# Second expert's weights loaded a phase earlier, its first matrix split in halves and its tokens transposed inside the first expert's first product

## The chip, the cores and the metric

One core of a Trainium2 chip runs the whole program. The metric is the device time of one execution in microseconds (us); the time of a kernel is the median of its runs.

## The reference, cut to what matters

A cross attention is added to `x` (32 batches of 256 tokens, width D = 256). Behind it stands a layer of E = 16 experts. Every expert takes the 512 tokens of the 8192 whose router logit for it is highest, so every expert has the same amount of work:

```python
logits = xn @ router_weight.T + router_bias
_, idx = jax.lax.top_k(logits.T, top_k)                  # 16 x 512
xe = xn[idx]
h = jnp.einsum('ecd,efd->ecf', xe, fc1_weight) + fc1_bias[:, None, :]   # F = 1024
h = jax.nn.gelu(h, approximate=False)
y = jnp.einsum('ecf,edf->ecd', h, fc2_weight) + fc2_bias[:, None, :]
contrib = (y * gates[:, :, None]).reshape(-1, d)
output = jnp.zeros(...).at[flat_idx].add(contrib)        # scatter-add, gates normalised
```

## The kernel before, in words

The program is four phases, one block each, with all engines meeting between two blocks.

- `attention_phase` (to about 540 us of the span): attention, router logits, and a table of normalised rows in HBM.
- `search_phase` (L779, 540 to 632 us): VectorE (DVE) looks for every expert's threshold by bisection, with one small matmul per step. Beside it SyncE (SP) loads expert 0's two weight matrices (L818, L820), ScalarE (ACT) copies them to a rounded high part (`W1H`, `W2H`, L847), and GpSimd (POOL) subtracts to get the low part (`W1L`, `W2L`, L835). Each part is announced by a semaphore (`w1h_ready`, `w1l_ready`, and the same for w2).
- `slots_phase` (L976, to 716 us): from thresholds to lists of token indices. At its end POOL gathers the tokens and gates of experts 0 and 1 (`XG`, `G`, L1050, L1056).
- `expert_phase` (L1162, from 716 us): the 16 experts.

All products of the expert phase are made in three passes (high x high, low x high, high x low; `three`, L1451). For an expert e of the pair (i, u), e = 2i + u, TensorE (PE) does: `columns` (L1441), 8 transposes of the gathered tokens into `xt_bank`; `up` (L1456), the first product in KF = 8 groups f of 6 matmuls of 512 columns, group f using columns f*128 to f*128+127 of `W1H` and `W1L`, with four PSUM banks in turn; `down` (L1469), the second product, 96 matmuls of 256 columns. PE's order is written out at L1484: columns(0), up(0), columns(1), up(1), columns(2), down(0), and then up(e), columns(e+1), down(e-1) for each further expert.

The other engines follow orders of their own:

- ACT (L1394): `hidden` makes for each group f the GELU from PSUM (`HF`, L1421) and, one group later, the rounded copy of group f-1 (`HH`, L1415). Between the hidden parts of two experts stands `split_1(e)` (L1398), one copy of the whole `W1` (2048 elements per partition) to `W1H`, and, from expert 2 on, `split_2(e-1)` (L1404).
- DVE (L1279): `columns` (L1302) scales the transposed tokens to a high part `XTH` (L1306) and a low part `XTL` (L1310). `split_1` (L1290) makes `W1L` (L1294). `hidden` (L1321) subtracts for each group to get `HL` (L1326). `indices` (L1281) copies index lists for POOL, `keep_gates` (L1314) saves the gates, `contributions` (L1329) turns the second product into the scaled output rows. The written order at the start (L1359) is columns(0), keep_gates(0), hidden(0), split_1(1), indices(2), columns(1), keep_gates(1), hidden(1), and then `turn` (L1347) for each expert: split_1(e), indices(e+1), columns(e), contributions(e-2), keep_gates(e), split_2(e-1), hidden(e).
- SP (L1202): waits for `w1l_ready` and loads `W1` of expert 1 (L1206), two bias rows (L1217), `W2` of expert 1 (L1211), and then for each further expert load_1(e), load_2(e), load_b(e). One buffer holds the raw `W1`, one the raw `W2`: the load of the next expert waits until the low part of the last one is made.
- POOL (L1229): gathers the tokens of experts 2, 3, ... (L1238, L1242) and scatter-adds finished rows (L1253), in turn.

The three lines that hold PE back between up(0) and up(1) are, on PE,

```python
            pe.wait_ge(xt_ready, e + 1)
            pe.wait_ge(w1l_ready, e + 1)
```

and on ACT, ahead of the copy that `W1L` is made from,

```python
                act.wait_ge(h_done, KF * e)
```

Of the kernel before, what the change touches and what calls it, by code (L numbers as in the profile page):

```python
# [4 lines left out]
FP32 = mybir.dt.float32  # L5
# [5 lines left out]
ALU = mybir.AluOpType  # L11
ACT = mybir.ActivationFunctionType
AX = mybir.AxisListType

P = 128
B, S, D = 32, 256, 256
M = 120
H, DH = 16, 16
# [5 lines left out]
F = 1024  # L24
KF = F // P
# [753 lines left out]
def search_phase(nc, ctx, sem, bank, ident, L, probs, front, w1T, b1, w2T, nw, same_e, same_e_below, same_e16, zero_row):  # L779
# [36 lines left out]
    @block.sync  # L816
    def _(sp):
        sp.dma_start(front["W1"][:, :, :], w1T[0:1, :, :].rearrange("o (k p) f -> p (o k) f", p=P)) \  # L818
            .then_inc(front["w1_loaded"], 16)
        sp.dma_start(front["W2"][:, :, :], w2T[0:1, :, :].rearrange("o (k p) d -> p (o k) d", p=P)) \  # L820
            .then_inc(front["w2_loaded"], 16)
        sp.dma_start(front["NW"][:, :], nw).then_inc(front["c_loaded"], 16)
        sp.dma_start(front["B1"][:, :], b1).then_inc(front["c_loaded"], 16)

    @block.gpsimd
    def _(pool):

        pool.wait_ge(mx_ready, 1)
        pool.tensor_tensor(expl[:, :, :], L[:, :, :], mx[:, :, :].to_broadcast([P, NT, E]), ALU.subtract) \
            .then_inc(lx_ready, 1)  # L830
        pool.wait_ge(ex_ready, 1)
        sum_experts(pool, tree, expl, sum_ready)
        for w in ("1", "2"):
            pool.wait_ge(front[f"w{w}h_ready"], 1)
            pool.tensor_tensor(front[f"W{w}L"][:, :, :], front[f"W{w}"][:, :, :], front[f"W{w}H"][:, :, :].bitcast(FP32),  # L835
                               ALU.subtract).then_inc(front[f"w{w}l_ready"], 1)
        pool.wait_ge(rsm_ready, 1)
        pool.tensor_tensor(probs[:, :, :], expl[:, :, :], rsm[:, :, :].to_broadcast([P, NT, E]), ALU.mult) \
            .then_inc(probs_ready, 1)

    @block.scalar
    def _(act):
        act.wait_ge(lx_ready, 1)
        act.activation(expl[:, :, :], expl[:, :, :], ACT.Exp).then_inc(ex_ready, 1)
        for w in ("1", "2"):
            act.wait_ge(front[f"w{w}_loaded"], 16)
            act.activation(front[f"W{w}H"][:, :, :], front[f"W{w}"][:, :, :], ACT.Copy).then_inc(front[f"w{w}h_ready"], 1)  # L847

    @block.vector
    def _(dve):  # L850
# [311 lines left out]
def expert_phase(nc, ctx, sem, bank, ident, front, idx, gate_table, xn_table, w1T, w2T, b2, out):  # L1162
# [39 lines left out]
    @block.sync  # L1202
    def _(sp):
        def load_1(e):
            sp.wait_ge(w1l_ready, e)
            sp.dma_start(W1[:, :, :], w1T[bass.ds(e, 1), :, :].rearrange("o (k p) f -> p (o k) f", p=P)) \  # L1206
                .then_inc(w1_loaded, 16)

        def load_2(e):
            sp.wait_ge(w2l_ready, e)  # L1210
            sp.dma_start(W2[:, :, :], w2T[bass.ds(e, 1), :, :].rearrange("o (k p) d -> p (o k) d", p=P)) \  # L1211
                .then_inc(w2_loaded, 16)

        def load_b(e, u, first=False):
            if not first:
                sp.wait_ge(y0_ready, e - 1)
            sp.dma_start(B2[u][:, :], b2[bass.ds(e, 1), :].to_broadcast([P, D])).then_inc(b2_loaded[u], 16)  # L1217

        load_1(1)
        load_b(0, 0, True)  # L1220
        load_b(1, 1, True)
        load_2(1)
        with sp.Fori(1, E // 2) as i:
            for u in range(2):
                load_1(2 * i + u)
                load_2(2 * i + u)
                load_b(2 * i + u, u)
# [52 lines left out]
    def _(dve):  # L1280
# [6 lines left out]
            dve.tensor_copy(II[u][:, :], idx[:, bass.ds(e, 1), 0, :].rearrange("p o g -> p (o g)"))  # L1287
            dve.tensor_copy(IG[u][:, :], idx[:, bass.ds(e, 1), 2, :].rearrange("p o g -> p (o g)")).then_inc(idx_ready, 1)  # L1288

        def split_1(e, first=False):  # L1290
            dve.wait_ge(w1h_ready, e + 1)
            if not first:
                dve.wait_ge(h_done, KF * e)
            dve.tensor_tensor(W1L[:, :, :], W1[:, :, :], W1H[:, :, :].bitcast(FP32), ALU.subtract).then_inc(w1l_ready, 1)  # L1294

        def split_2(e, first=False):
            dve.wait_ge(w2h_ready, e + 1)
# [20 lines left out]
            dve.wait_ge(gates_gathered[u], 16 * GT * (i + 1))  # L1318
            dve.tensor_copy(GK[u][:, :], G[u][:, :]).then_inc(gk_ready, 1)

        def hidden(i, u):  # L1321

            e = 2 * i + u
            for f in range(KF):
                dve.wait_ge(hh_ready, KF * e + (f + 1))
                dve.tensor_tensor(HL[u][:, f, :], HF[f % 4][:, :], HH[u][:, f, :].bitcast(FP32), ALU.subtract) \  # L1326
                    .then_inc(hl_ready, 1)
# [19 lines left out]
        def turn(i, u, ahead=True, first=False):  # L1347

            e = 2 * i + u
            split_1(e)  # L1350
            if ahead:
                indices(i + u, 1 - u, isinstance(e, int) and e == 2)
            columns(i, u)
            contributions(i - 1, u, first)
            keep_gates(i, u)
            split_2(e - 1)
            hidden(i, u)

        dve.wait_ge(c_loaded, 32)  # L1359
        columns(0, 0)  # L1360
        keep_gates(0, 0)
        hidden(0, 0)
        split_1(1)
        for g in range(E // EG):
            dve.wait_ge(ids_moved[g], 16 * EG)
        indices(1, 0, True)
        columns(0, 1)
        keep_gates(0, 1)
        hidden(0, 1)
        turn(1, 0, first=True)  # L1370
# [24 lines left out]
    def _(act):  # L1395
        act.wait_ge(c_loaded, 32)

        def split_1(e, first=False):  # L1398
            act.wait_ge(w1_loaded, 16 * (e + 1))
            if not first:  # L1400
                act.wait_ge(h_done, KF * e)
            act.activation(W1H[:, :, :], W1[:, :, :], ACT.Copy).then_inc(w1h_ready, 1)  # L1402

        def split_2(e, first=False):  # L1404
            act.wait_ge(w2_loaded, 16 * (e + 1))
# [4 lines left out]
        def hidden(i, u, first):  # L1410
            e = 2 * i + u

            def high(f):
                act.wait_ge(hf_ready, KF * e + (f + 1))
                act.activation(HH[u][:, f, :], HF[f % 4][:, :], ACT.Copy).then_inc(hh_ready, 1)  # L1415

            for f in range(KF):
                act.wait_ge(h_done, KF * e + (f + 1))
                if not isinstance(e, int) or e > 0 or f >= 4:
                    act.wait_ge(hl_ready, KF * e + (f - 3))  # L1420
                act.activation(HF[f % 4][:, :], h_bank[f % 4][:, :], ACT.Gelu,  # L1421
                               bias=B1[:, bass.ds(KF * e + f, 1)]).then_inc(hf_ready, 1)
                if f == 0 and not first:
                    act.wait_ge(y_done, e - 1)
                if f:
                    high(f - 1)
            high(KF - 1)

        hidden(0, 0, True)
        split_1(1)  # L1430
        hidden(0, 1, True)
        with act.Fori(1, E // 2) as i:
            for u in range(2):
                split_1(2 * i + u)
                split_2(2 * i + (u - 1))
                hidden(i, u, False)
        split_2(E - 1)
# [2 lines left out]
    def _(pe):  # L1440
# [12 lines left out]
            pe.matmul(o, wh, xl, start=False, stop=False)  # L1453
            return pe.matmul(o, wl, xh, start=False, stop=last)  # L1454

        def up(i, u, first):  # L1456
            e = 2 * i + u
            pe.wait_ge(xt_ready, e + 1)
            pe.wait_ge(w1l_ready, e + 1)
            for f in range(KF):  # L1460
                if not first or f >= 4:
                    pe.wait_ge(hf_ready, KF * e + (f - 3))
                for k in range(KD):
                    w = slice(f * P, (f + 1) * P)
# [17 lines left out]
            ins.then_inc(y_done, 1)  # L1482

        columns(0, 0, True)  # L1484
        up(0, 0, True)
        columns(0, 1, False)
        up(0, 1, False)
        columns(1, 0, False)
        down(0, 0, True)
# [74 lines left out]
```

## Time and profile before

| | us |
|---|---|
| median of 3 runs | 1132.67 |
| lowest, highest | 1127.72, 1132.79 |
| the profiled execution, its own time | 1131.91 |
| its span, first to last instruction | 1129.9 |
| PE busy in the span | 910.2 (81%) |
| DVE busy | 802.1 (71%) |
| POOL busy | 593.0 (52%) |
| ACT busy | 512.5 (45%) |

The profiled execution lies 2.0 us above its span and 0.76 us below the median. In the page's forty slices of 28 us each, PE stands at nine tenths through the attention, is near idle in the search, and is at nine tenths again from slice 28 to the end; the granted clock of TensorE is at half speed in between. A row of a timeline gives start, duration, engine, line, operation, output and inputs, the number of instructions merged, and in brackets how long the engine had been idle before and what ended that. Matmuls overlap in the records, so their pace is read from start to start, not from the duration of one. A row of a table by windows gives the stretch and its length, then the busy time of PE, of PE's weight loads, of DVE, ACT and POOL (with instruction counts), the granted clock as a share of 2.4 GHz, the share of the DMA engines and GB/s.

### The profile page before, as it was taken

The page shows a single profiled execution, that of the slowest core. Times are in us where ns is not written, and L with a number is a line of the kernel's source. Part 1 is how long each engine was busy: PE and PEld are TensorE (multiplying, and loading weights), DVE is VectorE, ACT ScalarE, POOL GpSimd, SP SyncE. Part 2 cuts the span into 40 slices and gives each one's busy share as a digit, 9 for nine tenths or more (in the row PEclk, how much of TensorE's full clock was granted, in tenths as well). Part 3 has the DMA queues.
Part 4 walks back from the last instruction along what each step waited for, and adds up shares of the span by engine and source line. Part 5 has one row for each costly group of instructions (what it writes and reads, how often), then busy time and mean ns, then how long its engine had stood idle before and what let it go on. Part 6 is the DMA issues. An engine that isn't in the chain of part 4 may idle for free. (4 is left out here: it accounts for less than half of the span.)

```text
span 1129.9 us, 22145 instructions
## 1 busy us (share of the span) xinstructions
PE 910.2 (81%) x7028; PEld 730.0 (65%) x7028; DVE 802.1 (71%) x1586; ACT 512.5 (45%) x872; POOL 593.0 (52%) x558
## 2 busy tenths in 40 slices
PE   4899999999999999986100054779999999999984
PEld 3566666666766666754000054669888999889974
DVE  4677888888888888872799899356666566665742
ACT  1545565555555655552100112354566545665440
POOL 4245566556655665554500218125677756767524
PEclk9889999999999999996555555789999999999997
DMA  4345555555555555632200001214456654455423
GB/s 157 126 157 186 201 193 187 209 212 198 187 203 199 192 186 211 213 140 84 78 0 0 0 22 39 87 57 117 126 130 159 161 121 130 127 166 153 122 61 37
DMA packets 110948, 150.68 MB, mean 133 GB/s; under 512 B 22453, under 2 KB 80053, under 8 KB 110905
## 3 DMA queue, kind: packets, MB, share of 16 engines
q1 hardware_dynamic: 96568, 133.29, 34.1%
q0 software_dynamic: 14336, 16.82, 8.5%
q8 instruction: 26, 0.43, 0.2%
q14 instruction: 18, 0.14, 0.1%
HBM read 57.67 MB, written 25.69 MB: 74 GB/s over the span
## 5 line engine op out<-in xcount | busy, mean ns | idle before, releaser
L525 DVE TENSOR_REDUCE NM<-bank 128x4 f32<-128x480 f32 x256 | 159.7, 656 | 55.1 <-PE bank L635 54.9
L368 ACT ACTIVATE PT<-bank 120x512 f32<-120x512 f32 x256 | 139.1, 595 | 66.4 <-PE bank L660 65.7
L310 POOL TENSOR_SCALAR XN<-X,mv,rstd 128x256 f32<-128x256 f32 x128 | 155.4, 1222 | 6.9 <-POOL rstd L305 6.1
L1452 PE MATMUL bank<-W2H,HH 128*128 128x256 f32 x512 | 145.9, 285 | 5.7 <-DVE Y L1339 5.7
L1453 PE MATMUL bank<-W2L,HH 128*128 128x256 f32 x512 | 144.5, 282 | 0.0
L1454 PE MATMUL bank<-W2H,HL 128*128 128x256 f32 x512 | 144.5, 282 | 0.0
L1326 DVE TENSOR_TENSOR HL<-HF,HH 128x512 fp32r<-128x512 f32 x128 | 86.6, 691 | 70.0 <-ACT HH L1415 69.4
L1253 POOL DMA_INDIRECT out_dram<-C,IO x60 | 102.9, 1714 | 45.6 <-DVE C L1344 28.0
L1452 PE MATMUL bank<-XTH,W1H 128*128 128x512 f32 x256 | 103.9, 406 | 11.6 <-DVE XTL L1310 11.6
L635 PEld LDWEIGHTS bank<-KX,QX 128*128 128x128 f32 x512 | 73.0, 195 | 61.7 <-issue 29.0
L478 DVE RECIPROCAL RR<-RC 128x256 f32<-128x256 f32 x64 | 111.3, 1741 | 1.6 <-DMA RC<-PVS 1.5
L635 PE MATMUL bank<-KX,QX 128*128 128x240 f32 x512 | 104.2, 317 | 9.6 <-issue 4.6
L1238 POOL DMA_INDIRECT XG<-xn_table,II x56 | 54.2, 969 | 106.2 <-DVE IG L1288 93.4
L343 POOL TENSOR_TENSOR XB<-X,bp_sb 128x512 f32<-128x512 f32 x32 | 40.5, 1265 | 124.9 <-DVE X L536 124.9
L1421 ACT ACTIVATE HF<-bank,B 128x512 f32<-128x512 f32 x128 | 87.9, 687 | 34.3 <-PE bank L1454 32.6
L1454 PE MATMUL bank<-XTH,W1L 128*128 128x512 f32 x256 | 102.3, 400 | 0.0
L1453 PE MATMUL bank<-XTL,W1H 128*128 128x512 f32 x256 | 102.1, 399 | 0.0
L1452 PEld LDWEIGHTS bank<-W2H,HH 128*128 128x128 f32 x512 | 97.5, 190 | 5.9 <-DVE Y L1339 5.9
L1453 PEld LDWEIGHTS bank<-W2L,HH 128*128 128x128 f32 x512 | 97.5, 190 | 0.0
L1454 PEld LDWEIGHTS bank<-W2H,HL 128*128 128x128 f32 x512 | 97.4, 190 | 0.0
L681 PE MATMUL bank<-PT,VA 120*32 120x256 f32 x1024 | 84.0, 400 | 0.2 <-ACT PT L368 0.2
L1242 POOL DMA_INDIRECT G<-gate_table,IG x56 | 74.3, 1327 | 17.1 <-issue 16.8
(156 smaller groups left out, 1849.3 us busy)
## 6 DMA issues: line engine op xcount, KB each, us to landing
QX<-QH SPq DMA_DIRECT2D x64, 256.0 KB
W<-w1T_dram SPq DMA_DIRECT2D x16, 1024.0 KB, 8.7
W<-w2T_dram SPq DMA_DIRECT2D x16, 1024.0 KB, 5.6
KX<-KH SPq DMA_DIRECT2D x64, 240.0 KB, 2.3
X<-x_dram SPq DMA_DIRECT2D x32, 256.0 KB, 2.8
QX<-QL SPq DMA_DIRECT2D x32, 256.0 KB
RC<-PVS SPq DMA_DIRECT2D x32, 256.0 KB, 2.4
OC<-PVS SPq DMA_DIRECT2D x32, 256.0 KB, 2.6
```

Of the source, the lines that this page charges most:

```text
L310: ins = pool.tensor_scalar(dst[:, t, :], src[:, t, :], mv[:, t, 0:1], rstd[:, t:t + 1], ALU.subtract, ALU.mult)
L368: act.activation(PT[u][0:M, HE * k:HE * (k + 1), :], score_bank[k % 2][0:M, :], ACT.Exp, scale=SCALE) \
L478: dve.reciprocal(RR[:, g, :], RC[:, g, :]).then_inc(rr_ready, 1)
L525: dve.tensor_reduce(NM[u][:, t, :].rearrange("p (f n e) -> p n e f", n=HN, e=HE)[:, n, :, :], smax_bank[q % 2][:, 0:4 * M].rearrange("p (e ...
L635: ins = pe.matmul(smax_bank[q % 2][:, e * 2 * M:(e + 1) * 2 * M], QX[u][:, HE * n + e, t * P:(t + 1) * P], KX[u][:, n, :, e, :], start=Tru ...
L681: ins = pe.matmul(pv_bank[k // 2][2 * DH * c4:2 * DH * (c4 + 1), (k % 2) * S:(k % 2 + 1) * S], VA[u][0:M, h, :, :].rearrange("p d o -> p ( ...
L1253: pool.indirect_dma_start(out=out, in_=C[u][:, g, :], in_offset=None, compute_op=ALU.add, out_offset=bass.IndirectOffsetOnAxis(ap=IO[u][:, ...
L1326: dve.tensor_tensor(HL[u][:, f, :], HF[f % 4][:, :], HH[u][:, f, :].bitcast(FP32), ALU.subtract) \
L1421: act.activation(HF[f % 4][:, :], h_bank[f % 4][:, :], ACT.Gelu, bias=B1[:, bass.ds(KF * e + f, 1)]).then_inc(hf_ready, 1)
L1452: pe.matmul(o, wh, xh, start=first, stop=False)
L1453: pe.matmul(o, wh, xl, start=False, stop=False)
L1454: return pe.matmul(o, wl, xh, start=False, stop=last)
```

## The change

`W1` and `W2` of expert 1 are loaded at the end of SP's list in the search phase, as soon as the low parts of expert 0 are made, and no longer at the start of the expert phase. `w1h_ready` and `w1l_ready` now count halves, two per expert. In the expert phase `split_1` works on one half of the columns of `W1` at a time, on ACT and on DVE, and the first half needs only the first four groups of the product before. In `up`, PE waits for the first half ahead of group 0 and for the second ahead of group 4. On the first expert alone, PE does columns(1) between groups 3 and 4 of up(0); DVE does its columns(1) ahead of `HL` of group 4 and the first half of split_1(1) ahead of `HL` of group 7; ACT does its first half behind `HF` of group 6 and `HH` of group 5. From expert 2 on the two halves follow one another where the one split stood.

```diff
@@ search_phase, SP
+        sp.wait_ge(front["w1l_ready"], 2)
+        sp.dma_start(front["W1"][:, :, :], w1T[1:2, :, :].rearrange("o (k p) f -> p (o k) f", p=P)) \
+            .then_inc(front["w1_loaded"], 16)
+        sp.wait_ge(front["w2l_ready"], 1)
+        sp.dma_start(front["W2"][:, :, :], w2T[1:2, :, :].rearrange("o (k p) d -> p (o k) d", p=P)) \
+            .then_inc(front["w2_loaded"], 16)
@@ search_phase, POOL and ACT
-        for w in ("1", "2"):
-            pool.wait_ge(front[f"w{w}h_ready"], 1)
+        for w, parts in (("1", 2), ("2", 1)):
+            pool.wait_ge(front[f"w{w}h_ready"], parts)
...
@@ expert_phase, SP
-            sp.wait_ge(w1l_ready, e)
+            sp.wait_ge(w1l_ready, 2 * e)
...
-        load_1(1)
         load_b(0, 0, True)
         load_b(1, 1, True)
-        load_2(1)
@@ expert_phase, DVE
-        def split_1(e, first=False):
-            dve.wait_ge(w1h_ready, e + 1)
-            if not first:
-                dve.wait_ge(h_done, KF * e)
-            dve.tensor_tensor(W1L[:, :, :], W1[:, :, :], W1H[:, :, :].bitcast(FP32), ALU.subtract).then_inc(w1l_ready, 1)
+        def split_1(e, half):
+            fs = slice(F // 2 * half, F // 2 * (half + 1))
+            dve.wait_ge(w1h_ready, 2 * e + half + 1)
+            dve.wait_ge(h_done, KF * e - KF // 2 * (1 - half))
+            dve.tensor_tensor(W1L[:, :, fs], W1[:, :, fs], W1H[:, :, fs].bitcast(FP32), ALU.subtract).then_inc(w1l_ready, 1)
...
-        def hidden(i, u):
+        def hidden(i, u, first=False):
             for f in range(KF):
+                if first and f == KF // 2:
+                    columns(0, 1)
+                if first and f == KF - 1:
+                    split_1(1, 0)
...
-            split_1(e)
+            split_1(e, 0)
+            split_1(e, 1)
...
         columns(0, 0)
+        hidden(0, 0, True)
+        split_1(1, 1)
         keep_gates(0, 0)
-        hidden(0, 0)
-        split_1(1)
         for g in range(E // EG):
             dve.wait_ge(ids_moved[g], 16 * EG)
         indices(1, 0, True)
-        columns(0, 1)
         keep_gates(0, 1)
         hidden(0, 1)
@@ expert_phase, ACT
+        def split_1(e, half):
+            fs = slice(F // 2 * half, F // 2 * (half + 1))
             act.wait_ge(w1_loaded, 16 * (e + 1))
+            act.wait_ge(h_done, KF * e - KF // 2 * (1 - half))
+            act.activation(W1H[:, :, fs], W1[:, :, fs], ACT.Copy).then_inc(w1h_ready, 1)
...
                 if f:
                     high(f - 1)
+                if first and e == 0 and f == KF - 2:
+                    split_1(1, 0)
             high(KF - 1)
...
         hidden(0, 0, True)
-        split_1(1)
+        split_1(1, 1)
         hidden(0, 1, True)
@@ expert_phase, PE
-        def up(i, u, first):
+        def up(i, u, first, mid=False):
             pe.wait_ge(xt_ready, e + 1)
-            pe.wait_ge(w1l_ready, e + 1)
             for f in range(KF):
+                if f % (KF // 2) == 0:
+                    pe.wait_ge(w1l_ready, 2 * e + 2 * f // KF + 1)
+                if mid and f == KF // 2:
+                    columns(0, 1, False)
...
-        up(0, 0, True)
-        columns(0, 1, False)
+        up(0, 0, True, mid=True)
```

## Rows read from the trace of the kernel before

**Rows 1.** Table by windows, two stretches of the expert phase (columns as told above).
```profile
735.40:743.40 8.00, 0.08 (x1) 0.08 (x1) 6.59 (x10) 2.64 (x3) 1.74 (x2) 0.69 0.23 55
...
757.10:1097.60 340.50, 339.91 (x2225) 308.44 (x2223) 218.18 (x337) 189.08 (x255) 217.63 (x160) 1.00 0.51 131
```

**Rows 2.** Chain that ended last, 740 to 744 us: start, us, what.
```profile
740.51 1.32 DVE XTH L1306 x2
...
741.86 1.42 DVE XTL L1310 x2
...
743.32 0.80 PE bank L1452
```

**Rows 3.** Timeline of SyncE: the two loads of W1 for experts 1 and 2.
```profile
716.51 0.39 SPq L1206 DMA_DIRECT2D W<-w1T_dram  x1
...
740.53 0.41 SPq L1206 DMA_DIRECT2D W<-w1T_dram  x1
```

**Rows 4.** Timeline of ScalarE, inside and behind the first expert's product.
```profile
728.91 0.69 ACT L1421 ACTIVATE HF<-bank,B 128x512 f32<-128x512 f32 x1 [0.19 <-PE bank L1454]
729.50 0.62 ACT L1415 ACTIVATE HH<-HF 128x512 fp32r<-128x512 f32 x1
...
736.14 1.90 ACT L1402 ACTIVATE W1H<-W 128x2048 fp32r<-128x2048 f32 x1
```

**Rows 5.** Timeline of VectorE behind the first expert's product.
```profile
735.75 1.29 DVE L1326 TENSOR_TENSOR HL<-HF,HH 128x512 fp32r<-128x512 f32 x2 [0.70 <-ACT HH L1415]
738.07 2.29 DVE L1294 TENSOR_TENSOR W1L<-W,W1H 128x2048 fp32r<-128x2048 f32 x1 [1.02 <-ACT W1H L1402]
```

**Rows 6.** Timeline of TensorE: starts of up(0) and up(1), pace at either clock.
```profile
721.52 0.79 PE L1452 MATMUL bank<-XTH,W1H 128*128 128x512 f32 x1 [3.02 <-DVE XTL L1310]
...
734.08 0.39 PE L1454 MATMUL bank<-XTH,W1L 128*128 128x512 f32 x1
734.31 1.04 PE L1448 MATMUL bank<-ident,XG 128*128 128x128 f32 x8
...
743.92 0.63 PE L1453 MATMUL bank<-XTL,W1H 128*128 128x512 f32 x1
744.34 0.63 PE L1454 MATMUL bank<-XTH,W1L 128*128 128x512 f32 x1
```

**Rows 7.** Table by windows: short stretches in which the granted clock changes.
```profile
724.00:725.00 1.00, 1.00 (x5) 0.76 (x4) 0.00 (x0) 0.47 (x1) 0.00 (x0) 0.59 1.07 370
...
738.00:740.00 2.00, 0.00 (x0) 0.00 (x0) 1.93 (x1) 0.04 (x1) 0.00 (x0) 0.62 0.02 4
...
748.00:749.00 1.00, 1.00 (x4) 0.76 (x4) 0.00 (x0) 0.15 (x1) 0.69 (x2) 0.64 0.02 1
...
1097.00:1098.00 1.00, 0.67 (x6) 0.47 (x4) 0.00 (x0) 0.24 (x1) 0.00 (x0) 1.00 0.00 0
...
1100.00:1101.00 1.00, 0.00 (x0) 0.00 (x0) 1.00 (x1) 0.00 (x0) 0.00 (x0) 0.65 0.00 0
...
1116.00:1117.00 1.00, 0.76 (x7) 0.56 (x5) 0.20 (x1) 0.00 (x0) 0.98 (x1) 1.00 0.00 0
...
1120.00:1121.00 1.00, 0.00 (x0) 0.00 (x0) 0.00 (x0) 0.00 (x0) 0.80 (x1) 0.89 0.49 74
```

**Rows 8.** Timeline of GpSimd: last token gather for expert 2.
```profile
745.11 0.95 POOL L1238 DMA_INDIRECT XG<-xn_table,II  x1 [0.30 <-issue]
```

**Rows 9.** Page's list of DMA issues: count and median us to landing.
```profile
XG<-xn_table,II POOLq DMA_INDIRECT x56, 2.8
```

**Rows 10.** Chain that ended last, 792 to 817 us: around W1 of expert 4.
```profile
792.90 1.30 DVE Y L1339 x2
...
799.54 9.90 DMA W<-w1T_dram
...
816.05 0.75 DVE XTL L1310
```

**Rows 11.** Table by windows: the expert period that holds the start of up(4).
```profile
804.00:828.30 24.30, 23.71 (x154) 21.27 (x153) 15.49 (x24) 13.48 (x18) 15.71 (x12) 1.00 0.55 144
```

More of the change, by code:

```diff
@@ L832, in _ @@
         sum_experts(pool, tree, expl, sum_ready)
-        for w in ("1", "2"):
-            pool.wait_ge(front[f"w{w}h_ready"], 1)
+        for w, parts in (("1", 2), ("2", 1)):
+            pool.wait_ge(front[f"w{w}h_ready"], parts)
             pool.tensor_tensor(front[f"W{w}L"][:, :, :], front[f"W{w}"][:, :, :], front[f"W{w}H"][:, :, :].bitcast(FP32),
-                               ALU.subtract).then_inc(front[f"w{w}l_ready"], 1)
+                               ALU.subtract).then_inc(front[f"w{w}l_ready"], parts)
         pool.wait_ge(rsm_ready, 1)
@@ L844, in _ @@
         act.activation(expl[:, :, :], expl[:, :, :], ACT.Exp).then_inc(ex_ready, 1)
-        for w in ("1", "2"):
+        for w, parts in (("1", 2), ("2", 1)):
             act.wait_ge(front[f"w{w}_loaded"], 16)
-            act.activation(front[f"W{w}H"][:, :, :], front[f"W{w}"][:, :, :], ACT.Copy).then_inc(front[f"w{w}h_ready"], 1)
+            act.activation(front[f"W{w}H"][:, :, :], front[f"W{w}"][:, :, :], ACT.Copy).then_inc(front[f"w{w}h_ready"], parts)
     @block.vector
@@ L1396, in _ @@
         act.wait_ge(c_loaded, 32)
-        def split_1(e, first=False):
+        def split_1(e, half):
+            fs = slice(F // 2 * half, F // 2 * (half + 1))
             act.wait_ge(w1_loaded, 16 * (e + 1))
-            if not first:
-                act.wait_ge(h_done, KF * e)
-            act.activation(W1H[:, :, :], W1[:, :, :], ACT.Copy).then_inc(w1h_ready, 1)
+            act.wait_ge(h_done, KF * e - KF // 2 * (1 - half))
+            act.activation(W1H[:, :, fs], W1[:, :, fs], ACT.Copy).then_inc(w1h_ready, 1)
         def split_2(e, first=False):
@@ L1433, in _ @@
             for u in range(2):
-                split_1(2 * i + u)
+                split_1(2 * i + u, 0)
+                split_1(2 * i + u, 1)
                 split_2(2 * i + (u - 1))
```

## The prediction

> **What bounds the kernel now.** I read the page's slices first, then a table by windows for the expert phase, then the chain of waits around the one hole in it, then the timelines of the engines there. From the start of the columns of expert 2 to the end of the second product of expert 13, PE is busy 339.91 of 340.50 us at full clock [rows 1]: nothing that happens on another engine there can gain more than the missing 0.59 us, and what PE starts earlier ends earlier by the same amount. Behind it comes a tail (last splits, last two second products, last scatters) that hangs on PE's end and is not edited, so it moves along rigidly. What is open is the hole between up(0) and up(1): PE idle for 8.0 us, from 735.35 to 743.32 [rows 1, 2, 6]. The chain through it is on ACT and DVE: behind the last rounded copy of the hidden part W1H starts at 736.14 and takes 1.90, W1L 2.29 from 738.07, and then XTH and XTL end at 743.28 [rows 2, 4, 5]. The hole has a second price. PE goes at 0.23 us per 512-column matmul before it and 0.42 behind it [rows 6]: the granted clock fell to the lower of its levels (1.2 GHz) in the idle time and came back to 2.4 GHz 5.4 us after the restart [rows 7]. up(1) is 48 matmuls, 11.2 us at the upper level; it took 743.32 to 757.07, 13.75 us, so 2.55 us went to the clock.
>
> **The early load.** W1 of expert 1 is issued at 716.51, and ACT's copy of it starts at 736.14 straight behind other ACT work, with no wait for a DMA [rows 3, 4]. The load was in time by a wide margin; moving it gains nothing by itself, and up to the same on the other side: in the search SP has nothing queued behind it but the block's end. W2 of expert 1 is used much later still. Two loads of 1 MB now run beside DVE's search loop, 90 us ahead of their use. I book 0, with +0.5 us as the far bound, for the case that a DVE step is held up somewhere. The SP queue at the start of the expert phase gets shorter by the same two issues; the bias rows come earlier and nobody waits for them.
>
> **The transposes inside up(0).** The same 8 transposes, about 0.9 us, move from behind group 7 to between groups 3 and 4. They don't vanish, they delay groups 4 to 7 by 0.9 us: PE ends up(0) at the same 735.2 instead of 734.3 plus transposes. Their input was gathered before the phase began. Cost 0. The gain is that DVE's 2.8 us of XTH and XTL can lie inside up(0).
>
> **The new chain, step by step,** on the clock of the trace of before. ACT: HF of group 3 starts at 728.91 and HH of group 2 behind it [rows 4]; each further group comes 1.4 us later, and groups 4 to 7 another 0.9 us later, so HF4 at 731.2, HF5 at 732.6, HF6 at 734.0. HH3 stands behind HF4 in ACT's order and ends at 732.4. HH5 ends at 735.2. There the first half of W1H is put. Its price from the two shapes seen, 0.62 us for 512 elements and 1.90 for 2048 [rows 4]: 0.62 + 1.28/3 = 1.05 us. It ends at 736.2; HF7 then ends at 736.9, HH6 at 737.4, HH7 at 738.0, the second half of W1H at 739.0. DVE: HL3 waits for HH3 and ends at 733.1, columns(1) take 2.8 us (XTH, then XTL, as in [rows 2]) to 736.0, HL4 and HL5 take 0.65 each [rows 5] to 737.3, HL6 waits for HH6 and ends at 738.1. The first half of W1L costs 0.69 + 1.6/3 = 1.22 us by the shapes 512 and 2048 [rows 5] (the second of the two HL alone is 0.69) and ends at 739.35. up(1) has its tokens from 736.0 and starts at 739.4, against 743.32: **gain 3.95 us**. HL7 and the second half follow on DVE to 741.2; PE asks for it at group 4, 5.6 us or more behind its restart, at 745.0 at the earliest. Hidden, by 3.8 us. The load of W1 for expert 2 waits for that second half, goes out at 741.3 instead of 740.53 [rows 3], and is needed at 753 at the earliest. Hidden.
>
> What is late next: DVE's copies of the indices for expert 2 come behind the second half and the gates, about 1 us later than before, and with them POOL's gathers. The last token gather starts at 746.1 instead of 745.11 and lands 2.8 us later [rows 8, 9], near 749. PE wants these tokens behind up(1), at 750.6 at the earliest. Hidden, but by 1.7 us only.
>
> **The clock.** The hole does not close; it shrinks from 8.0 to 4.1 us (735.25 to 739.4). Whether the clock falls in it decides the next term. Two-level averages give the moment of a fall or rise inside a row. Falls: last matmul at 735.35, fall at 738.5; 1097.67 and 1100.3; 1116.76 and 1120.8 [rows 6, 7], so 3.1, 2.6 and 4.0 us behind the last work. All three would lie within a stop of 4.1 us. Rises: restart at 721.52, rise at 724.8; restart at 743.32, rise at 748.7 [rows 2, 6, 7], so 3.3 and 5.4 us. I take it that the clock falls again. Each us at the lower level costs half a us, so 1.65 to 2.7, I take 2.1: **gain 0.45 us** (bounds -0.15 and +0.9). If the fall doesn't come, the gain is the whole 2.55.
> The Trainium skill (TensorE: Matmul & The Clock Gate, Part 1: The HAM clock gate) says that the number of slow matmuls at a start differs from run to run, and gives 6, 11 or 14 for one kernel. The extra 0.19 us of each slow matmul in this trace would make that, an estimate, 1.2 to 2.7 us instead of 1.65 to 2.7, and the gain of this term up to 1.4. It speaks for a wider band on one term and for nothing else; two rises in the trace can't show it.
>
> **The halves in the other experts.** ACT and DVE each issue one instruction more per expert. By the same shapes ACT pays 2.1 instead of 1.9 us and DVE 2.44 instead of 2.29. Both engines have over 7 us of slack in a period of 23.4 [rows 11]. But the chain W1H, W1L gets shorter, since DVE can start when the first half is copied: 1.05 + 1.22 + 1.22 = 3.5 us instead of 1.90 + 2.29 + 0.1 = 4.3. This matters at one place, where PE does wait: up(4) starts behind a load of W1 that took 9.90 us, the copies, and XTL to 816.80 [rows 10]; PE lost 0.59 us in that period [rows 11], all that is missing in [rows 1]. The chain gets 0.8 shorter: **gain 0.55 us** (bounds 0 and 0.59). PE's second wait in each `up` is for something made long before. Cost 0.
>
> **The sum.** 3.95 + 0.45 + 0.55 = 4.95 us. The profiled execution took 1131.91, so 1126.95. It lies 0.76 below the median of the three runs, which is 1132.67; against that median the same sum gives 1127.7. I forecast **1127.5**. About 0.5%, 5.7 us here, is what a measurement of this kernel can tell from no change (the runs shown spread over 5.1 us), so the forecast lies just inside that bound, which is at 1127.0.
>
> **Rivals.**
> *A, the clock holds.* Then the clock's term is 2.55 instead of 0.45, the sum 7.05, and the time 1132.67 - 7.05 = 1125.6. For it: one of three falls came only 4.0 us behind the last matmul, against a stop of 4.1 us, and a DVE chain shorter by a few tenths leaves no room for that one. Against it: the other two, 2.6 and 3.1 us. The cap is the gather for expert 2 (749 against 750.6). Chance 0.20.
> *B, the forecast,* clock falls once: 3.8 to 5.9 us of gain, 1126.5 to 1129.0. Chance 0.60.
> *C, the first half is not what PE waits for,* because some step of the new order is late: HL6 or HF7 in their queues, or both halves arriving together near 741.2. That is 1.85 us less; with a late rise of the clock, 4.95 - 1.85 - 0.6 = 2.5 us, and 1130.2. For it: DVE's order now holds eight things between HL3 and the second half, each behind ACT. Against it: each step ahead of the first half is a duration and an order read from rows. Chance 0.14.
> *D, slower.* W1's load for each expert from 4 on is the tightest recurring chain: from the end of a second product at 792.8 (DVE takes it up at 792.90) to the end of XTL at 816.80 are 24.0 us with a landing of 9.90 [rows 10], against a period of 23.4. Halves make it 23.2. With them POOL is told of the next indices 0.8 us sooner, and its gathers and scatters move nearer to W1's load. If that pushes the landing beyond about 10.1 us in every period, each us more costs a us in each of 12 experts; at 10.9 that is 0.8 x 12 = 9.6 us lost, net 4.7, and 1137.3. For it: 9.90 was seen once. Against it: that once only, since PE has no idle time in the later periods [rows 1, 11]. Chance 0.06.
>
> **How the numbers follow.** The predicted time is B's. The range takes B, A with a us below it for the scatter of runs, and the nearer part of C: 1124.3 to 1130.6; left out are D, the rest of C, and the far edge of A. Faster by over 0.5% (below 1127.0) is nearly all of A, 0.19, and a third of B, 0.20: 0.39. Slower by over 0.5% (above 1138.3) is the worse part of D and what I didn't think of: 0.06. The rest, 0.55, is within 0.5%.
>
> **What would show it.** In the trace of the changed kernel: no wait of ACT for W1 of expert 1 in either version; eight transposes near 729, XTH and XTL of expert 1 on DVE near 733 to 736; PE idle about 4 us ahead of up(1), released by W1L and not by XTL; a granted clock that falls once in it; up(1) over 13 us from its first matmul to its last if it fell, 11.2 if not; W1L in two pieces of 1.2 us; no idle time on PE ahead of up(4). I am wrong if the hole is closed or is above 5.5 us, if up(1) stops ahead of group 4, if columns(2) wait for their gather, or if PE shows idle time in the periods from expert 4 on.

## The result, and the profile after

| | before | changed |
|---|---|---|
| median of 6 runs each, us | 1130.68 | 1120.49 |
| lowest, highest | 1127.53, 1132.79 | 1117.99, 1122.78 |
| profiled execution, its span | 1131.91, 1129.9 | 1122.78, 1121.1 |
| first product of expert 0 starts | 721.52 | 716.64 |
| first product of expert 1 starts | 743.32 | 734.38 |
| transposes of expert 2 start | 757.07 | 748.46 |

The ratio is 0.9912 (95% interval 0.9888 to 0.9937): 9.9 us faster, where I had forecast a gain of 4.95 us and a time of 1127.5, with 1124.3 as the lowest. The six runs of the kernel before include the three that were known ahead of the prediction. Two more measurements of the changed kernel, further down, gave 0.9949 and 0.9935. All ratios are of fast runs: left out as slow are one run at 1153.5 us of the kernel before, beside e1 to e4, and one at 1670.82 us of e9.

The two profiles differ by 8.8 us of span. Of these, 4.9 lie ahead of the first product, in phases of which the change touches only SyncE's loads; 3.9 lie behind it. The chain that I had written out is there, step by step. TensorE's timeline of the kernel before has this row at the hole:

```profile
743.32 0.80 PE L1452 MATMUL bank<-XTH,W1H 128*128 128x512 f32 x1 [7.97 <-DVE XTL L1310]
```

TensorE of the changed kernel, timeline:

```profile
716.64 0.79 PE L1463 MATMUL bank<-XTH,W1H 128*128 128x512 f32 x1 [3.02 <-DVE XTL L1314]
...
723.89 1.04 PE L1459 MATMUL bank<-ident,XG 128*128 128x128 f32 x8
...
734.38 0.77 PE L1463 MATMUL bank<-XTH,W1H 128*128 128x512 f32 x1 [3.85 <-issue]
```

The hole of 7.97 us is now 3.85 us long. The trace puts no name to what ended it ("issue"); VectorE's timeline does, since the first half of `W1L` ends at 734.28:

```profile
727.61 0.69 DVE L1334 TENSOR_TENSOR HL<-HF,HH 128x512 fp32r<-128x512 f32 x1 [1.59 <-ACT HH L1423]
728.22 1.41 DVE L1310 TENSOR_SCALAR XTH<-bank,NW 128x512 fp32r<-128x512 f32 x2
729.66 1.41 DVE L1314 SCALAR_TENSOR_TENSOR XTL<-bank,NW,XTH 128x512 fp32r<-128x512 f32 x2
730.99 1.28 DVE L1334 TENSOR_TENSOR HL<-HF,HH 128x512 fp32r<-128x512 f32 x2
732.45 0.69 DVE L1334 TENSOR_TENSOR HL<-HF,HH 128x512 fp32r<-128x512 f32 x1 [0.18 <-ACT HH L1423]
733.06 1.22 DVE L1298 TENSOR_TENSOR W1L<-W,W1H 128x1024 fp32r<-128x1024 f32 x1
```

On the clock of before, which runs 4.88 us later, these are 733.1 for XTH, 735.9 for the end of XTL and 739.2 for the end of the half: the forecast had 733.1, 736.0 and 739.35. The halves have the durations worked out from [rows 4, 5], 1.22 us on VectorE and on ScalarE (its timeline)

```profile
730.28 1.05 ACT L1410 ACTIVATE W1H<-W 128x1024 fp32r<-128x1024 f32 x1
```

The loads of expert 1 went out in the search (SyncE's timeline), and nothing waited for them in either kernel:

```profile
552.07 0.38 SPq L825 DMA_DIRECT2D W<-w1T_dram  x1
556.52 0.38 SPq L828 DMA_DIRECT2D W<-w2T_dram  x1
```

By the table of windows the granted clock fell in the hole at 733.7 and rose at 740.6, so the product of expert 1 took 14.1 us (734.38 to 748.46), and behind it TensorE stands still for no more than 0.1 us, where [rows 1] had 0.59:

```profile
733.00:734.00 1.00, 0.00 (x0) 0.00 (x0) 1.00 (x2) 0.88 (x1) 0.00 (x0) 0.87 0.03 8
740.00:741.00 1.00, 1.00 (x5) 0.75 (x4) 0.00 (x0) 1.00 (x2) 0.69 (x2) 0.72 1.05 426
...
748.50:1088.60 340.10, 339.99 (x2225) 308.49 (x2223) 219.76 (x351) 190.24 (x270) 213.64 (x160) 1.00 0.50 131
```

So the question for the experiments is less the chain than the size: 9.9 us of measured gain, of which the profile shows 3.9 us behind the first product.

### The profile page after: what moved, and what is told of

Its sections match the earlier page's. It is cut to its first block and busy times, and to the rows that moved or that the text cites. A ratio compares the mean times of both kernels' runs of the same rounds, so it can differ in the third digit from the quotient of the medians.

```text
span 1121.1 us, 22237 instructions
## 1 busy us (share of the span) xinstructions
PE 907.5 (81%) x7028; PEld 727.0 (65%) x7028; DVE 797.9 (71%) x1601; ACT 513.5 (46%) x887; POOL 587.3 (52%) x558
## 5 line engine op out<-in xcount | busy, mean ns | idle before, releaser
L660 PE MATMUL bank<-QX,KX 64*120 64x256 f32 x512 | 64.6, 331 | 17.9 <-ACT PT L368 16.4
```

## The experiments

Every profile gives two numbers that matter here: when the first product starts, and how long it is from there to the end of the span. That second number is called the stretch below; it holds every edit but the moved loads and the counts of two semaphores. The ratio is to the kernel before, timed beside it.

| kernel | ratio (interval) | search starts | first product | from there to the end |
|---|---|---|---|---|
| before, first profile | | 540.6 | 721.5 | 408.4 |
| changed, first profile | 0.9912 (0.9888 to 0.9937) | 539.6 | 716.6 | 404.5 |
| e1 before | 1.0003 (0.9973 to 1.0033) | 541.5 | 732.1 | 417.5 |
| e2 loads only | 0.9994 (0.9966 to 1.0023) | 539.6 | 728.6 | 419.4 |
| e3 all but the loads | 0.9924 (0.9894 to 0.9955) | 545.0 | 732.2 | 407.3 |
| e4 transposes only | 0.9956 (0.993 to 0.9983) | 541.3 | 732.2 | 412.1 |
| e5 changed | 0.9949 (0.9923 to 0.9975) | 542.5 | 720.1 | 404.0 |
| e6 changed less transposes | 1.0008 (0.9981 to 1.0035) | 536.8 | 717.5 | 406.8 |
| e7 whole split from expert 2 on | 0.996 (0.9935 to 0.9986) | 538.1 | 716.2 | 404.4 |
| e8 fillers in the hole | 0.9935 (0.9908 to 0.9962) | 549.7 | 726.8 | 403.2 |
| e9 all of expert 1 earlier | 0.9919 (0.9889 to 0.9949) | 537.8 | 717.8 | 399.3 |
| e10 the same, late indices | 0.9908 (0.9874 to 0.9941) | 548.8 | 727.2 | 398.4 |
| e11 changed | 0.9935 (0.9911 to 0.9959) | 537.5 | 714.0 | 404.1 |
| e12 before, one run | | 550.4 | 727.7 | 408.9 |
| e13 loads only | 1.0005 (0.9977 to 1.0034) | 541.6 | 723.0 | 409.0 |
| e14 all but the loads | 0.9949 (0.992 to 0.9978) | 540.2 | 713.6 | 403.6 |
| e15 transposes only | 0.9993 (0.9966 to 1.002) | 538.0 | 720.6 | 406.4 |
| e16 before | 1.0017 (0.9993 to 1.0041) | 543.7 | 722.4 | 408.6 |

### First batch: which part, and is it the part ahead of the experts

e1 is the kernel before, unchanged.

> The kernel before, unchanged, for a second profile of the phases ahead of the experts. In the two profiles so far the first product starts 4.9 us earlier after the change (716.6 against 721.5), with 1.1 us of that at the end of the attention, 0.5 in the search and 3.3 in the phase of the slots; the chain edited in the expert phase gave 4.1 us more. Theory S (scatter: the phases ahead of the experts vary from execution to execution and the change has no part in it): ratio 1.000 within 0.002, and the first product starts anywhere between 716 and 722. Theory L (the change made the phases ahead shorter): ratio 1.000 too, but the first product starts at 721 to 722 again, with the slots phase within 0.5 us of the first profile.

e2, the loads alone (the diff leaves out the second load, which is moved in the same way):

```diff
+        sp.wait_ge(front["w1l_ready"], 1)
+        sp.dma_start(front["W1"]..., w1T[1:2, ...]).then_inc(front["w1_loaded"], 16)
...
-        load_1(1)
-        load_2(1)
```

> The kernel before with nothing but the two loads of the second expert moved into the search phase. Theory S: no change, ratio 0.999 to 1.001 (the copy of the weights never waited for its load). Theory L (early loads, or the shorter SyncE list, free something ahead of or at the start of the experts): 4 to 5 us faster, ratio about 0.996, with the first product starting near 717.

e3, the changed kernel with the two loads taken out of the search phase and put at the start of the expert phase again:

```diff
+        load_1(1)
         load_b(0, 0, True)
         load_b(1, 1, True)
+        load_2(1)
```

> The changed kernel with the two loads put back at the start of the expert phase. Theory S: as fast as the changed kernel, ratio 0.991 to 0.994 to the kernel before. Theory L: the 4 to 5 us of the early phases are lost, ratio 0.995 to 0.997. In both the hole of TensorE ahead of the second expert's first product is about 4 us.

e4, only the transposes and their scaling inside the first product:

```diff
+                if mid and f == KF // 2:
+                    columns(0, 1, False)
...
+                if first and f == KF // 2:
+                    columns(0, 1)
```

> The kernel before with only the second expert's transposes (and their scaling on VectorE) moved into the first product; its first matrix is still split whole and its loads stay. By the chain: the rounded copies of groups 4 to 7 run to about 737 on the clock of the first profile, the copy of the whole matrix takes 1.90 us and its low part 2.29, so the second product up starts near 741.3 against 743.3: 2.0 us from the hole, and with the scaling off the chain nothing else. Ratio 0.998 under theory S. Under a theory that the scaling was the only thing on the path, 2.8 us, ratio 0.9975.

This chip was slower for every kernel (the kernel before: median 1147.13). Two things in its profiles were new. While GpSimd gathered, TensorE's small matmuls of the slots phase stood still a dozen times for "issue", 10.2 us in e1. And behind the second product of expert 0 both ScalarE and VectorE started late, at the same moment, after a wait that the trace puts down to a "remote" releaser (ScalarE's and VectorE's timelines of e1):

```profile
784.54 1.92 ACT L1408 ACTIVATE W2H<-W 128x2048 fp32r<-128x2048 f32 x1 [13.32 <-remote]
```
```profile
784.54 1.29 DVE L1339 TENSOR_TENSOR Y<-bank,B 128x512 f32<-128x512 f32 x2 [7.82 <-remote]
```

TensorE had ended that product near 779.9. Two waits of TensorE in its timeline follow from it, the second since the load of `W1` for expert 3 stands behind these steps in the queue:

```profile
787.08 0.49 PE L1452 MATMUL bank<-XTH,W1H 128*128 128x512 f32 x1 [1.57 <-ACT HF L1421]
...
808.80 0.50 PE L1452 MATMUL bank<-XTH,W1H 128*128 128x512 f32 x1 [3.59 <-DVE XTL L1310]
```

The same stall was in e2 and e4. In e3 it came later and cost little. So of the 8.5 us of gain of e3 on this chip a part seems to be an escape from a stall that the profiles of the other chips don't have; with one profile of each kernel, it is not shown that the changed order is what avoids it. What the remote releaser is stays open: no experiment here bears on it. What does follow from the batch: the loads alone change nothing that can be measured (e2, 0.9994), and everything else without them gives 0.9924 (e3). The changed kernel itself was not run on this chip.

### Second batch: the halves, the clock

e5 is the changed kernel.

> The changed kernel again, for a second profile and beside the parts of it. Theory H (the gain lies in the expert phase: about 4 us of the hole, up to 4 us of stalls of ScalarE and VectorE in the periods of experts 2 and 3 that the changed order escapes, and on some executions the clock): ratio 0.990 to 0.994, from the start of the first product to the end of the span 405 to 408 us against 417 to 419 in the kernel before where those stalls show. Theory E (half of the gain lies ahead of the experts): the first product starts 4 us or more earlier than in the kernel before, and the rest of the span is only 4 us shorter.

e6, halves and loads, but the transposes of expert 1 back behind the first product, and their scaling back behind the index copies on VectorE (the diff shows TensorE's part):

```diff
-        up(0, 0, True, mid=True)
+        up(0, 0, True)
+        columns(0, 1, False)
```

> The changed kernel with the transposes of expert 1 back behind the first product (and the scaling back behind the index copies on VectorE): loads early, W1 in halves. By the chain the scaling, 2.8 us, is on the path again behind the second half of W1L (which then lies ahead of it), so the second product up starts 1.9 + 2.8 us later than in the changed kernel: near the time before, at 742.0 to 743 on the first clock, hole 6.5 to 8 us. Theory H, where the gain is in the hole: ratio 0.996 to 1.000 to the kernel before. If the halves in the periods of experts 2 and 3 are what counts: 0.993 to 0.996.

e7, one whole split from expert 2 on:

```diff
-                split_1(2 * i + u, 0)
-                split_1(2 * i + u, 1)
+                split_1_whole(2 * i + u)
```

> The changed kernel with W1 split whole from expert 2 on; halves for expert 1 alone. My prediction gave the halves from expert 2 on 0.55 us: ratio to the kernel before 0.991 to 0.993, the same as the changed kernel. If they are what keeps TensorE from waiting in the periods of experts 3 and 4 (3.6 us seen in the second profile of the kernel before), the ratio is 0.994 to 0.996 and a wait for the tokens of 2 to 4 us shows ahead of up(3) or up(4).

e8, work for TensorE in the hole:

```diff
         up(0, 0, True, mid=True)
+        for _ in range(32):
+            pe.transpose(y_bank[0][:, 0:P], ident[:, :], ident[:, :])
         up(0, 1, False)
```

> The changed kernel with 32 transposes of the identity into an unused bank in the hole ahead of up(1) (0.11 us each, 3.5 us in all; their result is never read). TensorE then idles only some 0.4 us there. If the clock falls in that hole, as I predicted, and costs 2 to 3 us: up(1) takes 11.2 us instead of 14.1, the clock shows no fall between the two products, and the kernel is 1.5 to 3 us faster than the changed one (0.9975 to 0.9985 of it). If the clock mostly holds there and the first profile of the changed kernel was unlucky: no faster than the changed one.

e5: ratio 0.9949, 5.8 us, and a stretch of 404.0 us. That is theory H's shorter stretch with less than theory H's ratio.

e6: no gain at all by the ratio, and the hole is 7.64 us. VectorE's timeline shows why the halves alone hardly shorten the hole: both are done at 736.4, but the scaling is then behind them.

```profile
733.48 1.22 DVE L1298 TENSOR_TENSOR W1L<-W,W1H 128x1024 fp32r<-128x1024 f32 x1
...
735.22 1.22 DVE L1298 TENSOR_TENSOR W1L<-W,W1H 128x1024 fp32r<-128x1024 f32 x1
...
738.00 1.41 DVE L1314 SCALAR_TENSOR_TENSOR XTL<-bank,NW,XTH 128x512 fp32r<-128x512 f32 x2
```

The stretch of e6 is 1.8 us shorter than in the kernel before all the same, 406.8 against 408.6. Of that 0.3 is the hole and 1.2 is up(1), 12.6 us against 13.8, since the clock rose sooner behind its first matmul in this one profile. A ratio with an interval of 3 us to either side can't show 1.8 us.

e7: the small wait ahead of up(4) is back, as TensorE's timeline has it, and is the only wait in its stretch that the changed kernel doesn't have:

```profile
806.94 0.49 PE L1471 MATMUL bank<-XTH,W1H 128*128 128x512 f32 x1 [0.55 <-DVE XTL L1319]
```

My prediction had 0.55 us for this term.

e8: with the fillers TensorE is idle for 0.36 us ahead of up(1), the clock stays at 2.4 GHz (the third number from the end of the row is its share), and up(1) takes 11.3 us:

```profile
745.40:756.80 11.40, 11.34 (x49) 9.13 (x50) 5.46 (x12) 7.93 (x13) 6.80 (x7) 1.00 0.43 138
```

So the hole is what makes the clock fall, and it costs 1.5 us (against 12.8 in e5) to 2.8 us (against 14.1 in the first profile). The stretch is 403.2 us, 0.8 us less than in e5 beside it. In the whole time it is at the edge of what could be measured: 0.9935 against 0.9949, with intervals that overlap.

### Third batch: closing the hole

e9 moves everything of expert 1 further ahead. After the path of VectorE above, three things had to go: the scaling and the first half ahead of more of the `HL`, and the gathers of expert 2, which my prediction had named as the cap.

```diff
-                if first and f == KF // 2:
+                if first and f == KF // 4:
                     columns(0, 1)
-                if first and f == KF - 1:
+                if first and f == KF // 2:
                     split_1(1, 0)
...
-                if first and e == 0 and f == KF - 2:
+                if first and e == 0 and f == KF // 2:
                     split_1(1, 0)
...
-                if mid and f == KF // 2:
+                if mid and f == KF // 4:
                     columns(0, 1, False)
...
         columns(0, 0)
+        keep_gates(0, 0)
+        for g in range(E // EG):
+            dve.wait_ge(ids_moved[g], 16 * EG)
+        indices(1, 0, True)
         hidden(0, 0, True)
...
```

The last lines are taken out of their old place behind `split_1(1, 1)`.

> The changed kernel with everything of expert 1 moved further ahead: its transposes behind group 1 of the first product, its scaling ahead of HL of group 2, the first half of W1H behind HF4 and HH3, the first half of W1L ahead of HL of group 4, and the index copies for expert 2 at the very start. Theory H (the path through the hole is ACT's and DVE's order and nothing else; the clock falls because of the hole): the first half is ready near 18 - 4 = 14 us behind the start of the first product, TensorE shows almost no idle time ahead of up(1), the clock does not fall, and from the start of the first product to the transposes of expert 2 it takes 25.5 to 27 us against 31.8 in the changed kernel and 35.5 before; ratio to the kernel before 0.988 to 0.991. If the clock falls for another reason than the hole: 2 to 3 us less.

e10 is e9 without this last part, the move of the gates and the indices. e11 is the changed kernel and e12 the kernel before, both unchanged.

> As the one before, but the index copies for expert 2 stay behind the second half of W1L, as in the changed kernel. By the cap named in my prediction GpSimd's gathers for expert 2 now land too late: told at about 24 us behind the start of the first product, the last one starts 5 us later and lands 2.8 us later, near 28.5, while TensorE is ready for them at 26. A wait of 2 to 3 us for a DMA ahead of the transposes of expert 2, which takes back as much of the gain; ratio 0.990 to 0.993.

> The changed kernel on the same chip as the two before, so that they can be set against it. Theory S of the first batch (what lay ahead of the first product was scatter, the expert phase gives 4 to 5 us): ratio 0.994 to 0.997 to the kernel before, as in the second measurement; from the start of the first product to the end of the span 403 to 405 us. If the first measurement (0.9912) was the true one: 0.990 to 0.993.

> The kernel before, one look on this chip. Theory S: the first product starts somewhere between 716 and 727 us, as in the profiles of kernels whose early phases are the same; from there to the end 408 to 409 us if ScalarE and VectorE do not stand still together behind the second product of expert 0, 413 or more if they do.

e9 closes the hole: on TensorE's timeline up(1) starts 0.17 us behind the last work, the clock stays up, and from the first product to the transposes of expert 2 are 26.4 us (717.82 to 744.25) against 31.8 in the changed kernel and 35.5 in the kernel before.

```profile
732.97 0.47 PE L1463 MATMUL bank<-XTH,W1H 128*128 128x512 f32 x1 [0.17 <-issue]
...
744.25 1.04 PE L1459 MATMUL bank<-ident,XG 128*128 128x128 f32 x8
```

From the first product to the end it takes 399.3 us, 4.9 less than the changed kernel. e10 was to lose 2 to 3 us of this to a gather that comes too late. The wait is there, but is 0.38 us:

```profile
753.05 1.09 PE L1459 MATMUL bank<-ident,XG 128*128 128x128 f32 x8 [0.38 <-DMA XG<-xn_table,II]
```

The second half of `W1L` was done 18 us behind the start of the first product, not 24, so the indices came earlier than I had reckoned. The ratios, 0.9919 and 0.9908 against 0.9935 for the changed kernel on the same chip, point the same way as the stretch, but their intervals overlap. By the stretch either version beats both kernels; by the whole time that it beats the kernel before is shown, that it beats the changed one is not.

### Fourth batch: scatter or loads

e13 is e2 again, e14 is e3, e15 is e4 and e16 is the kernel before, all on a chip whose profiles don't show the stall.

> Only the two loads moved. If the early loads shorten the phases ahead of the experts (the profiles with them start the first product at 714 to 727, mean 719.5, those without on the same kind of chip at 721.5 and 727.7): ratio 0.996 to 0.998 and a first product 3 us earlier than in the kernel without them. If all that is scatter: 0.999 to 1.001.

> Everything but the moved loads. If the early loads count for 3 us: ratio 0.996 to 0.998. If they count for nothing: the mean of the three measurements of the changed kernel, 0.993 within 0.0025, and at least the 0.996 that the edited stretch alone gives.

> Only the transposes inside the first product. Hole 6.0 us instead of 8.0 as in its first profile, so the stretch from the first product to the end is 2 us shorter, 406 to 407 us; ratio 0.998 if this kind of chip shows no stalls of ScalarE and VectorE, 0.996 if it does as the other did.

> The kernel before against itself: ratio 1.000; whatever it differs from that by is what one measurement with 5 rounds can be off by. A first product between 716 and 728 us, 408 to 409 us from there to the end.

The loads alone once more give nothing (1.0005), and all but the loads gives what the changed kernel gave on other chips (0.9949). The kernel before against itself came out at 1.0017. The transposes alone make the hole 5.98 us, as forecast (TensorE's timeline), and the stretch 2.2 us shorter; by the ratio that is nothing that can be told from zero, and the 0.9956 of e4 came on the chip with the stall.

```profile
740.29 0.77 PE L1453 MATMUL bank<-XTH,W1H 128*128 128x512 f32 x1 [5.98 <-issue]
```

The search phase takes 92.5 to 92.8 us in every profile but the first (93.2). Two other phases vary, with no regard to the kernel. The attention ends at 536.8 to 550.4 us. The slots phase, from the end of the search to the first product, takes 80.8 to 89.9 us on the chips without the stall, and 94.5 to 98.3 on the one with it; of the 4.9 us ahead of the first product in the first two profiles, 3.3 are there. So the first product starts at 713.6 to 727.7 on the chips without the stall. The stretch varies by 0.5 us for the kernel before (408.4, 408.9, 408.6) and for the changed one (404.5, 404.0, 404.1).

Both phases go with the granted clock. In the first 200 us it is 0.95 to 0.97 in the profiles whose attention ends by 543 us, 0.94 in the two that end it near 544 and 545, and 0.91 or 0.92 in the three that end it at 548.8 to 550.4; the correlation over all eighteen is -0.94. In the slots phase it is 0.61 in e14 (80.8 us) and 0.52 in e15 (89.9 us). That the clock makes the difference is not tested. Tables by windows, first 100 us of e9 and of e10:

```profile
0.00:100.00 100.00, 74.60 (x490) 52.34 (x490) 65.69 (x117) 41.88 (x85) 41.70 (x55) 0.95 0.47 160
```
```profile
0.00:100.00 100.00, 74.20 (x437) 51.70 (x438) 58.56 (x103) 37.72 (x76) 36.48 (x48) 0.86 0.41 140
```

## Why the prediction was wrong

**The early load: 0.** Right within what the runs can tell, by e2 (0.9994) and e13 (1.0005), whose intervals are 3 us to either side, and by their stretches.

**The chain: gain 3.95.** Right. The hole went from 7.97 to 3.85 us in each of the three profiles, 4.1 us, and XTH, XTL and the half lie within 0.2 us of the forecast. That VectorE's queue is the last one to hold the first half is read from the trace: ScalarE's half is done at 731.3, VectorE is busy with `HL` until it takes up its own half at 733.06, and TensorE restarts 0.1 us behind its end. e9 closes the hole by moving work on TensorE, ScalarE and VectorE at once, which fits this and shows that the order of the three is the cause, but does not single out VectorE. In the hole the gain isn't the sum of the parts: transposes alone 2.0 us, halves alone 0.3, both 4.1. Either one left alone puts the other on the path.

**The clock: falls, gain 0.45.** Right that it falls, in all three profiles, so rival A is out; e8 shows that the hole is the cause. Up(1) took 13.75, 13.8 and 13.8 us in the kernel before (first profile, e12, e16) and 14.1, 12.8 and 12.8 in the changed one, 0.55 us less on the mean. The reading behind it was less sure than it looked. I took all falls to come within a stop of 4.1 us. In e5 and e11 the fall came 4.7 and 4.5 us behind the last matmul, 0.9 and 0.7 us behind the restart. The table by windows of e5, where TensorE restarts at 739.10:

```profile
738.00:739.00 1.00, 0.00 (x0) 0.00 (x0) 1.00 (x2) 0.60 (x1) 0.00 (x0) 1.00 0.02 8
739.00:740.00 1.00, 0.90 (x4) 0.80 (x5) 1.00 (x2) 0.00 (x0) 0.00 (x0) 0.98 0.00 0
740.00:741.00 1.00, 1.00 (x4) 0.78 (x3) 1.00 (x5) 0.00 (x0) 0.00 (x0) 0.50 0.00 0
```

What I left out is that the first rise of the clock, in up(0), scatters as well: 3.3, 3.5 and 3.6 us behind its first matmul in the three profiles of before, 3.4, 6.2 and 5.9 in the changed kernel's. That took back about 0.8 us. The Trainium skill (TensorE: Matmul & The Clock Gate, Part 1: The HAM clock gate) says that the number of slow matmuls at a start varies from run to run; the trace agrees, by these numbers.

**The halves in the other experts: gain 0.55.** Right, by e7, and by the wait of 0.59, 0.72 and 0.59 us in the profiles of before that is absent in those of the changed kernel. From the transposes of expert 2 to the end it takes 0.5 us less.

**The sum: 4.95.** The stretch is 4.4 us shorter (408.6 to 404.2, three profiles each): 4.1 of the hole, 0.55 of up(1), 0.5 behind it, less 0.8 in up(0). Another 0.25 us lies outside the span: the time of a run is 2.0 us more than its span in the kernel before and 1.7 us more in the changed one. So the mechanism and its price held, and **the step that failed** is the next one, "How the numbers follow": "the range takes B, A with a us below it for the scatter of runs", together with the sum's "against that median the same sum gives 1127.7". I took the median of three runs, 1132.67, as the level of the kernel before, though those three spread over 5.1 us. Three more runs of it made the median 1130.68, and later medians were 1128.96, 1127.68 and 1128.59 on chips without the stall. And I gave one us to the scatter of the result, while two phases ahead of the edit, the attention and the slots phase, move by up to 14 and 9 us from profile to profile. The range was also put together with a slip: B's gain of at most 5.9 us ends at 1126.8 and not at 1126.5, and the upper bounds read from rows, 3.95, 0.9 and 0.59, add up to 5.4.

The three measurements of the changed kernel are 0.9912, 0.9949 and 0.9935; weighed by their intervals they give 0.9932, 7.7 us with 1.6 us to either side. The first of them lies 2.2 us beyond that. That it did is luck as far as is known.

**What stays open.** 7.7 us stand against 4.4 in the stretch and 0.25 outside the span, which leaves 3 us for which no part is found. By the intervals of the three measurements that is nearly four standard errors; by the spread of the three ratios among one another, whose standard error is 1.2 us, it is two and a half. So chance is neither shown nor excluded. It isn't the loads: e14, without them, gave 0.9949 too. Nor does the granted clock, which is on record for every run, account for it. Within the kernel before, a longer run goes with a lower mean clock (correlation -0.80 beside e5 and -0.83 beside e14, 35 runs each; about 0.9 us for each 0.001). But the changed kernel's runs had a mean clock 0.0014, 0.0028 and 0.0025 above their neighbours in e5, e11 and e14 (one run with 0.857 left out), and the edit alone makes about 0.0020, since its stretch has 25 us at the lower clock against 30. The difference is worth under 1 us. Executions that stall as on the second chip could be it, if some of the unprofiled runs of the kernel before had that. No profile of it on the other chips shows the stall.

Rival C (the first half isn't what TensorE waits for) is out by the trace, where TensorE restarts 0.1 us behind it, rival D (the load of `W1` landing too late) by the periods without a wait. A rival that I hadn't thought of is a stall of two engines at once in the second period: on one chip the stretch is 10.2 us shorter in e3 than in e1, and the edit explains 4.4 of that.

## What to carry to other kernels

A chain read from one trace can be right to 0.2 us while the time of the kernel is off by 5, if the phases that aren't edited scatter more than the edit is worth: judge such an edit by the stretch from its start to the end of the span, in several profiles, and widen the range by the spread of the runs shown. When two edits lie on the same path, test each without the other: here one alone closed 2.0 us of the hole, the other 0.3, and both 4.1. A hole on TensorE cost its length and then the slow matmuls behind it, so the last step, which closed it, paid more than the step before: 4.9 us of stretch for 3.7 us of hole.

## What the runs showed that I had not expected

- The attention of the same code ended between 536.8 and 550.4 us in eighteen profiles, whatever was changed behind it, and later where the granted clock of its first 200 us was lower.
- One chip ran every kernel 1.6% slower (median 1147.13 against 1128 to 1131), with TensorE standing still a dozen times (e1) for nothing that the profile names while GpSimd issued gathers, and, in three of its four profiles, with ScalarE and VectorE starting at the same instant (784.54 in e1), some 4.6 us behind the end of the product that both seemed to wait for.
- Thirty-two transposes whose result nobody reads held the clock over a hole of 3.9 us, and made the product behind it 1.5 to 2.8 us shorter.
